# A two-layer AdaLN/MoE/BitLinear kernel on one core: another order of work in its opening, gate statistics on another engine, and the clip ahead of the low half in group 0

## The reference

```python
# layer 0
y   = einsum('bct,bcd->bdt', x, weights[condition])   # 64x64 matrix per sequence: "mix"
h   = relu(layernorm(y @ gw1.T + gb1) * gamma + beta) # 32 wide
top = top_k(h @ gw2.T + gb2, 2)                       # 2 of 8 experts; dropped if over capacity
out = y @ weight.T + sum_e w_e * (y @ A_e) @ B_e / 16 # main product and low-rank part
x   = x + out
# layer 1
z     = einsum('bsi,boi->bso', x, weight1[adapter])   # one of 8 matrices per sequence
q(w)  = round(clip(w / (mean|w| + eps), -1, 1)) * mean|w|
out   = ((z @ q(w_gate).T) * (z @ q(w_up).T)) @ q(w_down).T
x     = x + out
```

## Time and profile before

| | us |
|---|---|
| median of 3 runs (1402.75 to 1405.18) | 1404.03 |
| the profiled execution | 1402.66 |
| its span, first to last instruction | 1401.0 |
| VectorE busy | 751.2 (54%) |
| ScalarE busy | 370.4 (26%) |

### The profile page before, as it was taken

The page is one execution under the profiler, slowest core; times in us unless marked ns, Lnnn a source line. Parts: engine busy times, 40 slices in busy tenths (PEclk is TensorE's granted clock), DMA queues, the critical chain, the costliest instruction groups (busy, mean ns, idle before and its releaser), DMA issues.

```text
span 1401.0 us, 24489 instructions
## 1 busy us (share of the span) xinstructions
PE 1334.8 (95%) x8864; PEld 851.6 (61%) x8865; DVE 751.2 (54%) x1159; ACT 370.4 (26%) x401; POOL 157.5 (11%) x115
## 2 busy tenths in 40 slices
PE   5889899979999989999999999999999999999998
PEld 5874444434444444555544688854788844888843
DVE  5467555343355556888855255573355572455521
ACT  3332443100111155777730011120011110111100
POOL 3200000000011000000000023320133210122310
PEclk9999999989999999999999999999999999999999
DMA  8744999979998847999864743353644445543354
GB/s 219 166 122 181 376 410 419 313 240 218 308 252 265 220 146 265 342 337 337 285 231 162 248 141 138 147 219 131 221 155 157 147 184 184 211 157 144 131 202 143
DMA packets 174336, 310.67 MB, mean 222 GB/s; under 512 B 99360, under 2 KB 131360, under 8 KB 166464
## 3 DMA queue, kind: packets, MB, share of 16 engines
q1 hardware_dynamic: 158352, 254.04, 55.6%
q10 hardware_dynamic: 11440, 32.69, 6.3%
q0 software_dynamic: 4480, 23.07, 4.7%
HBM read 220.78 MB, written 68.03 MB: 206 GB/s over the span
## 4 chain that ended last, share of the span: by engine, by line
PE 68%; DMA 9%; DVE 7%; issue 5%; SPq 5%; ACT 4%; POOL 1%; POOLq 0%; ACTq 0%; DVEq 0%
PE pair L982 26%; PE pair L1019 15%; PE pair L854 12%; PE pair L946 6%; DMA region_q<-in_L_cond_weight 5%; PE pair L770 4%; DMA region_q<-wb_scratch 2%; DMA region_w<-in_L_ffn_w_gate 2%; ACT region_q L1202 2%; SPq L474 2%; PE pair L737 1%; PE pair L667 1%; PE pair L725 1%; PE pair L900 1%; DVE region_q L1656 1%
## 5 line engine op out<-in xcount | busy, mean ns | idle before, releaser
L982 PE MATMUL pair<-act_t,region_q 128*128 128x256 f16 x3696 | 404.0, 273 | 0.0
L982 PEld LDWEIGHTS pair<-act_t,region_q 128*128 128x128 f16 x3696 | 361.6, 98 | 42.6 <-issue 0.2
L1019 PE MATMUL pair<-region_q,region_w 128*128 128x512 f16 x1232 | 267.6, 379 | 4.4 <-DMA region_q<-wb_scratch 4.1
L1019 PEld LDWEIGHTS pair<-region_q,region_w 128*128 128x128 f16 x1232 | 120.0, 98 | 150.7 <-DMA region_q<-wb_scratch 5.5
L652 POOL TENSOR_TENSOR region_w<-region_q,region_w 128x1792 f32 (+1 forms) x33 | 118.4, 3589 | 742.7 <-ACT region_w L1239 742.7
L854 PE MATMUL pair<-region_w,act_t 128*128 x816 | 178.9, 379 | 1.8 <-DVE region_q L1566 1.8
L770 PE MATMUL pair<-region_w,act_t 128*128 128x512 f16 x768 | 174.3, 385 | 0.0
L946 PE MATMUL pair<-act_t,region_q 128*128 128x512 f16 x704 | 158.6, 384 | 2.6 <-issue 2.6
L854 PEld LDWEIGHTS pair<-region_w,act_t 128*128 x816 | 79.8, 98 | 94.7 <-issue 2.5
L770 PEld LDWEIGHTS pair<-region_w,act_t 128*128 (+1 forms) x768 | 76.1, 99 | 89.6 <-issue 4.7
L1245 ACT ACTIVATE region_q<-pair 128x512 f32<-128x512 f32 x33 | 19.7, 597 | 402.5 <-PE pair L982 402.5
(11 more groups left out here) (185 smaller groups left out, 1016.8 us busy)
## 6 DMA issues: line engine op xcount, KB each, us to landing
region_q<-wa_scratch SPq DMA_DIRECT2D x33, 1792.0 KB, 7.3
region_q<-wb_scratch SPq DMA_DIRECT2D x28, 1408.0 KB, 6.1
region_q<-in_L_cond_weight SPq DMA_DIRECT2D x40, 512.0 KB, 8.8
w1s_scratch<-region_q ACTq DMA_DIRECT2D x40, 512.0 KB, 8.3
wa_scratch<-region_q SPq DMA_DIRECT2D x22, 896.0 KB, 6.0
region_q<-in_x SPq DMA_DIRECT2D x64, 256.0 KB, 4.8
region_w<-in_L_ffn_w_gate SPq DMA_DIRECT2D x16, 688.0 KB, 5.5
wb_scratch<-region_q SPq DMA_DIRECT2D x11, 896.0 KB, 4.1
```

What stands on the lines that cost most here:

```text
L982: mm = pe.matmul(bank(s_bank, b)[:, (1 - h) * HALF:(2 - h) * HALF], ring_a[s][:, h, o_a, k], moving[a], start=(opens and h == 1 and k == 0 ...
L1019: mm = pe.matmul(bank(s_bank, b), iop[:, a, p, o_a, tp * P:(tp + 1) * P], ring_b[r][:, p], start=(opens and p == 0 and a == 0), stop=(not ...
```

## The change

It has six parts.

1. SyncE issues one factor load ahead of the index instead of eight, the other seven behind x tiles 2, 4, 6 and 8. Four index entries are fetched by one `fields` instead of one `field` each, on SyncE for x and on GpSimd for the condition matrices.
2. The w0 blocks alternate between the third and fourth PSUM pair, the mixes between the first two as before but starting in the second; the turned gate weight goes into half of the first pair.
3. TensorE makes the mixes of tiles 0 to 11 ahead of the first gate product. The 16 gate products stand behind mixes 11 to 15 (table `GATES`) in four banks of the third and fourth pair. The halves of the factors move to tile 10. The gate arithmetic starts at tile 12.
4. The statistics of w_gate: 18 pieces of 1280 columns (the last 256; 640 KB and 128 KB) instead of 16 of 1376, loaded from ScalarE's queue from tile 9 on and summed by ScalarE (Abs with an accumulated sum): 9 of them behind the mixes of tiles 11 to 15 (table `SUMS`), 9 among the rank-0 parts. VectorE's 16 reductions and SyncE's 16 loads in the layer-0 loop are gone.
5. ScalarE's order in rank 0: parts 0 to 3 with a sum each, Exp, then four times store o, part o + 4, sum; then the other stores. The weighted factors are written in place of the unweighted ones.
6. In group 0 VectorE's `quantize` stands ahead of `low_inter`.

The core of the diff:

```diff
+LORA_AFTER = {2: (1,), 4: (2, 3), 6: (4, 5), 8: (6, 7)}
+            def load_mix(t, perm):
+                for s in range(2):
+                    wait_if(sp, y_done, t + s - 3)
+                    slot = (t + s) % 4
+                    for h in range(2):
+                        sp.dma_start(mix_nat[slot][h * SEQ:(h + 1) * SEQ, :], x_rows[ds(perm[2 * s + h] * SEQ, SEQ), :])\
+                          .then_inc(mix_loaded[slot], 16)
...
-            for k in range(KC):
-                sp.dma_start(lora_a_nat[:, k], lora_a[:, k * P:(k + 1) * P, :].rearrange("e i r -> i e r"))\
-                  .then_inc(lora_loaded, 16)
+            load_lora(0)
             sp.wait_ge(index_ready, 1)
...
+            for t in range(0, NT, 2):
+                load_mix(t, fields(sp, F_PERM + 2 * t, 4, NB - 1))
+                if t < 4:
+                    for r in range(4 + t, 6 + t):
+                        load_w(w0[r * P:(r + 1) * P, :], r, r % 4)
+                for k in LORA_AFTER.get(t, ()):
+                    load_lora(k)
...
                     load_pair(x_nat[s], x_loaded[s], t)
-                    for p in (GATE_LOADS[t] if isinstance(t, int) else ()):
-                        load_gate(p, p % 2, stat_gate)
...
 # ScalarE
+            def sum_gate(p):
+                cols = piece_cols(p)
+                tile = stat_gate[p % 2][:, 0:cols.stop - cols.start]
+                act.wait_ge(gate_loaded[p % 2], 16 * (p // 2) + 16)
+                act.activation(tile, tile, ACT.Abs, accum_out=stat_g[:, p:p + 1]).then_inc(gate_summed, 1)
+                if p + 2 < NPIECE_G:
+                    load_gate(p + 2)
...
-            for o in range(2, 6):
-                store_w(o, o % 4)
-                rank0_part(o + 2)
+            for o in range(4):
+                store_w(o, o)
+                rank0_part(o + 4)
+                sum_gate(13 + o)
+            sum_gate(17)
+            for o in range(4, 7):
+                store_w(o, o - 4)
...
 # VectorE
-            for t in range(10, NT):
-                residual(t, t % 2, pair[t % 2])
-                for p in GATE_PIECES[t]:
-                    v.wait_ge(gate_loaded[p % 2], 16 * (p // 2) + 16)
-                    v.tensor_reduce(stat_g[:, p:p + 1], stat_gate[p % 2], X, ALU.add,
-                                    apply_absolute_value=True).then_inc(gate_summed, 1)
-                prep_low(t // 2, t)
-                low_x1(t)
...
                     product(m - 1, (c - 1) % 2, 2 * i + (c - 1) // 2, (c - 1) // 2 % 2)
+                    quantize(m + 2, c % 2, 2 * i + c // 2 + 1)
                     if c % 2 == 1:
                         low_inter(2 * i + (c - 3) // 2, (c - 3) // 2 % 2)
-                    quantize(m + 2, c % 2, 2 * i + c // 2 + 1)
```

More of the change, by code:

```diff
@@ L727, in mix, with gate @@
                 mm.then_inc(y_done, 1)
[L730 removed]
+            def gate(t):
                 pe.wait_ge(y_low, t + 1)
[L732 to L733 removed]
+                wait_if(pe, tmp_copied, t - 3)
+                dst = gate_bank(t)
                 n = 0
@@ L740, in gate @@
                 mm.then_inc(tmp_done, 1)
-            pe.wait_ge(w_low, 3)
-            for t in range(4):
-                mix(t, t, t % 2, 32)
-                if t > 0:
-                    prep_w0(t + 3)
-            pe.wait_ge(ag_low, 2)
-            gate(0, 0)
-            done = 1
-            for t in range(4, 8):
-                mix(t, t - 4, t % 2, 64)
-                if t == 4:
-                    prep_w0(7)
-                for _ in range(1 + t % 2):
-                    gate(done, done % 2)
-                    done += 1
-            with loop(pe, 2, 4) as i:
-                for c in range(4):
-                    mix(4 * i + c, c, c % 2, 32 * i + 32)
-                    gate(4 * i + c - 1, (c - 1) % 2)
-            gate(NT - 1, 1)
+            for t in range(NT):
+                if t == 1:
+                    pe.wait_ge(ag_low, 1)
+                    pe.wait_ge(index_ready, INDEX_ALL)
+                mix(t, t % 4, (t + 1) % 2, 32 * (t // 4 + 1))
+                if t == 0:
+                    prep_w0(2)
+                    prep_w0(3)
+                elif t < 5:
+                    prep_w0(t + 3)
+                for n in GATES.get(t, ()):
+                    if n == 0:
+                        pe.wait_ge(w_low, NPREP0)
+                        pe.wait_ge(ag_low, 2)
+                    gate(n)
             def main(t, s, q):
@@ new lines, in _ @@
+            small = ((g1b[:, :], gb1), (lng[:, :], ln_g), (lnb[:, :], ln_b), (g2w, gw2.rearrange("e h -> (e h)")),
+                     (g2b[:, :], gb2))
+            for t in range(NT):
+                for n in GATES.get(t - 1, ()):
+                    tmp_part(n)
+                if t == 13:
+                    gate_sqrt(0)
+                y_part(t, (t + 1) % 2)
+                if t == 0:
+                    high_w0(2)
+                    high_w0(3)
+                elif t < 5:
+                    high_w0(t + 3)
+                if 2 <= t < 7:
+                    act.dma_start(small[t - 2][0], small[t - 2][1].partition_broadcast(P)).then_inc(small_loaded, 16)
+                if t in (9, 10):
+                    load_gate(t - 9)
+                if t == 10:
+                    act.wait_ge(lora_loaded, 16 * KC)
+                    high(ag[:, 0, :, 0:ER], lora_a_nat.rearrange("p k e r -> p k (e r)"), WGT_SCALE)\
+                        .then_inc(ag_high, 1)
+                if t >= 14:
+                    gate_sqrt(t - 13)
+                for p in SUMS.get(t, ()):
+                    sum_gate(p)
@@ L1118, in _ @@
+            for n in GATES[NT - 1]:
+                tmp_part(n)
             act.wait_ge(lora_b_loaded, 16)
```

204 lines of the change are left out of this document (78 added, 126 removed).

## The result

The changed kernel takes 1399.19 us (median of 20 runs, 1393.61 to 1405.67), the kernel before beside it 1405.07 us (20 runs, 1401.38 to 1408.18): a ratio of 0.9959, 95% interval 0.9946 to 0.9971, so faster by 5.9 us. The forecast was 1382. The direction holds, the size does not: 17 us are missing. The profiled execution took 1401.02 us, its span is 1399.3.

A forecast was written before the change was run, and what follows sets the result against it. TensorE, busy 95% of the span, was taken as the bound, leaving holes and slow stretches to win. Opening 1.9 + end of layer 0 10.5 + clip 9 = 21.4 us off 1402.66, then adjusted to 1382; eight in ten 1364 to 1399.

The forecast's parts named there:

- the front of the opening: Loads and mixes before the gate products: gates open at 46.3 us, main products start (M) at 81 instead of 100.56.
- SyncE's early issue: Opening, SyncE's queue: factor loads behind x and one index fetch for four start x at about 7.5 us instead of 16.67.
- the gate stretch: TensorE's 16 gate products and mixes 12 to 15, from gate opening to main products: 33.9 us, plus 1 for slow clock.
- the sign that it would be wrong: Opening: holes in the gate stretch, with ScalarE waiting for gate pieces with y halves behind it, would refute the forecast.
- Rival B: Opening: the front is bound by transfer, not by issue; main products start at 91, time 1392 us; chance 17%.
- My second bound: Opening's transfer: 4 MB of weights and 5.5 MB of x at 300 GB/s take 32 us, from 3 us on.
- The tail: ScalarE's queue behind Exp: four serial rounds of 6.9 us (store landing 4.4), lora(0) at 127.8, TensorE idle 14.8 us.
- The estimate of 3.2 us: ScalarE's tail: a 512 KB store lands in 3.2 us, a round takes 5.7, final time 4.8 us lower than forecast.
- The end of layer 0: Layer-0 loop's end: without reductions and gate loads the 7.46 us hole and 3.0 us of slow clock go, 10.5 us.
- The clip: Second layer's first group: VectorE's clip ahead of the low half closes eight holes and shrinks the ninth, 9 us.
- rival C: Second layer's first group: the clip gains nothing, as ScalarE's round is late for another reason; 1391 us; chance 8%.
- Slow clock: TensorE behind the idle stretch before lora(0): the clock lowered by idling costs 3.0 us.

The follow-up runs named there:

- experiment 5: Changed kernel with x tiles 4 to 15 of the opening loading only their first 512 columns, half the bytes (other data): 1386.23 us, ratio 0.9863 to the kernel before.
- experiment 4: Changed kernel with w0 blocks 6 and 7 asked for behind x tiles 4 and 5 instead of ahead: 1397.29 us, ratio 0.9956 to the kernel before.
- experiment 2: Changed kernel with all eight factor loads ahead of the index, as before, none among the x loads: 1400.28 us, ratio 0.9972 to the kernel before.
- experiment 6: Changed kernel with all 18 gate sums but only the first two gate pieces loaded (other data): 1379.98 us, ratio 0.9819 to the kernel before.
- experiment 9: Changed kernel with loads of gate pieces 14 to 17 issued right behind the stores instead of right ahead: 1391.02 us, ratio 0.9898 to the kernel before.
- experiment 1: Kernel before with only the clip moved ahead of the low half in the FFN's group 0: 1393.79 us, ratio 0.9921 to the kernel before.
- experiment 11: Changed kernel with all gate sums and their loads in layer 0 and rank 0's first four stores ahead of the halves: 1395.06 us, ratio 0.9929.
- 13: Changed kernel with sums 0 to 3 in the gate products, 4 to 17 in layer 0's tiles 11 to 14, stores ahead: 1374.51 us, ratio 0.9793.
- experiment 3: Changed kernel with factor loads reading rows of 512 bytes from w0 instead of 64-byte rows (other data): 1398.17 us, ratio 0.9963 to the kernel before.
- experiment 10: Changed kernel with all 18 gate sums and their piece loads moved from the opening into layer 0: 1398.25 us, ratio 0.9952 to the kernel before.

## Why the prediction was wrong

**The step that failed: the front of the opening.** It put M at 81, with a lower end of 76 and an upper of 91; it is 97.49, outside both. That is 16.5 of the 19.8 us by which lora(0) missed 127.8. It was built on two sums, and both came out too low: SyncE's issue times (x tile 10 at 36 us, in fact 47.60) and the transfer at 300 GB/s.

By position: mix 0 is 3.9 us late, released by the loads of the condition matrices (3.67 us of waiting); mix 4 is 11.2 us late (34.24 against 23); the gates open 12.9 us late (59.18 against 46.3). So nearly all of it is lost by mix 4, ahead of the mixes 5 to 11 that the change put together. Of the 12.9 us, 7.2 go when x has half the bytes (experiment 5), so they are transfer. The other 5.7 are not the pace of the later mixes, for in experiment 5 these take 20.7 us from mix 4 to the gates, fewer than the forecast's 23.3. They stand ahead of mix 4: its x leaves only when SyncE's stop at w0 block 6 is over. But without that stop (experiment 4) the wait turns up at a w0 block and the gates open no sooner, so what these 5.7 us hang on stays open. SyncE's early issue, on which the sum was built, brings nothing that can be told at M (experiment 2).

The rest of the lateness of M, 3.6 us, is in the gate stretch: 38.31 us in place of 33.9, less the 1.0 of slow clock that the forecast had added: ScalarE waits for gate pieces with copies behind it. The prediction named that as the sign that it would be wrong, and experiment 6 shows it: without the loads the stretch is the forecast 33.9. It is so too with all the pieces but half of x (experiment 5), so the pieces are late only beside the whole of x.

Rival B had the mechanism and the sign, with too small a price. My second bound took 300 GB/s from one window of ten microseconds; over 32 to 50 us the engines moved 136 to 209 at a share of 0.89 to 1.13. A rate read in one good window is not a forecast.

**The tail: right in mechanism, short in size.** The rounds behind Exp came as described, one hole before lora(0), the halves released by the stores. From the first store (113.53, M + 16.0, forecast M + 15.2) the four rounds took 31.4 us against 27.6, landings of 4.6, 7.6, 5.5 and 3.0 against the 4.4 taken. That is 3.4 us at lora(0). I had seen the piece ahead of the store and priced it at about 1 us a round; by experiment 9 it is 2.4 us a round. The estimate of 3.2 us for such a store, worked out in the prediction from the Trainium skill (DMA: Bandwidth & Descriptors, "Anatomy of one DMA — SWDGE (gpsimd) path") and given there for another issue path, is below all of these landings but the last; the measurement decides.

**The end of layer 0: right.** 10.5 forecast; about 10 by the positions of residual 3 and of layer 1's start. The hole that goes is 7.46; experiment 1 shows that it stays when the rest of the change is absent.

**The clip: right, a little small.** 9 forecast, 11.1 alone, about 10 in the change. All nine holes but one closed; rival C is out.

**Slow clock.** Forecast 3.0 us behind the idle stretch. The granted clock was 0.59 and 0.50 in the windows 130:140 and 140:150, and residual 3's hole moved 2.0 us more than lora(0): somewhat less than forecast.

**The whole.** Without any loss of the piece loads the change gives 1380, two from the forecast; but that is chance, for there a front 12 us late stands beside a tail 11 us better than forecast.

## What to carry to other kernels

Before moving a stream of loads, put its bytes over the windows of the place where they go: where the engines already stand at their greatest rate (420 GB/s here), or where one queue holds stores that an engine waits for, they cost dearly (18 us given back for 11.3 MB, which take 27 us at that rate); where the rate has fallen they were free. The place alone was worth 20.6 us (experiment 11 against 13, both with the stores ahead). In a queue of one engine, issue what somebody waits for first and what can wait behind it: that order alone was worth 8 to 11 us. And when an issue is moved forward, ask for the rate over the whole stretch, not for that of one good window.

## What the runs showed of the hardware that was not expected

- A DMA busy share near 1.0 says little of the rate: it stood at 0.93 with 136 GB/s (32 to 38 us) and at 1.03 with 417 (210 to 230 us), both of the changed kernel. Whether the factor loads' rows of 64 bytes have a part in it is not shown (experiment 3 moved M by 3.5 us, within the scatter of profiles). Why the opening, with loads of much the same size in one busy queue where layer 0 has two, stays so far below 417 was not settled.
- A 512 KB store alone in its queue is not fast either: the second one behind Exp was waited for 4.4 us in experiment 6 and 6.07 us in experiment 10, with no gate piece anywhere near, only w1's loads in SyncE's queue.
- ScalarE's sum of 1280 columns is two instructions, 1.27 and 0.19 us, and the traces show no table load between it and the copies.
